# A graph-attention and graph-kernel pipeline over 16 pairs of batches: prologue in another order, x buffers by parity, last tiles finished one by one

## The reference

```python
def layer0(x, wq, wk, adj, bm):                     # attention over the 512 columns
    q, k = einsum('c,bcn->bn', wq, x), einsum('c,bcn->bn', wk, x)
    s = leaky(q[:, None, :] + k[:, :, None], 0.01)
    att = softmax(s, axis=-1)                       # 512 x 512 of each batch
    agg = einsum('bcn,bmn->bcm', x, att)
    return relu(einsum('oc,bcm->bom', adj, agg) + bm)

def layer1(h, adj, W_lang, W_grav, W_V, W_O):       # kernel over the 256 rows
    z_l, z_g, v = h @ W_lang.T, h @ W_grav.T, h @ W_V.T
    A_l = relu(cosine(z_l, z_l)) * not_eye          # 256 x 256 of each batch
    A_g = exp(-dist2(z_g, z_g) / (2 * sigma**2)) * not_eye
    K = w_l * rows_to_one(A_l * adj) + (1 - w_l) * rows_to_one(A_g * adj)
    return (K @ v) @ W_O.T

x = layernorm(x + layer0(x))
out = layernorm(x + layer1(x))
```

## Time and profile before

| what | value |
|---|---|
| median of three runs | 1048.47 us (1047.57 to 1049.12) |
| the profiled execution's own time | 1045.15 us |
| its span | 1043.4 us |
| TensorE busy | 1014.2 us, 97% |
| VectorE, ScalarE, GpSimd busy | 792.3 us (76%), 654.6 us (63%), 385.6 us (37%) |
| granted TensorE clock over the span | 0.996 of full speed |
| start to step 1 (0 to 143.31): TensorE busy | 124.88 us |
| steps 1 to 15 up to the last residual (143.31 to 1032.79): TensorE busy | 889.35 of 889.48 us |
| last residual to the end (1032.79 to 1043.40): TensorE busy | 0 of 10.61 us |

### The profile page before, as it was taken

The page is one execution under the profiler, slowest core; times in us unless marked ns, Lnnn a source line. Parts: engine busy times, 40 slices in busy tenths (PEclk is TensorE's granted clock), DMA queues, the critical chain, the costliest instruction groups (busy, mean ns, idle before and its releaser), DMA issues.

```text
span 1043.4 us, 19673 instructions
## 1 busy us (share of the span) xinstructions
PE 1014.2 (97%) x7189; PEld 695.5 (67%) x7189; DVE 792.3 (76%) x2318; ACT 654.6 (63%) x1267; POOL 385.6 (37%) x340
## 2 busy tenths in 40 slices
PE   7888999999999999999999999999999999999995
PEld 4465848577584857758485775848577584857662
DVE  5775776878787687878768787876878787787756
ACT  2658576665857666585766658576665857666432
POOL 0335334262533426253242625324262532424200
PEclk9999999999999999999999999999999999999998
DMA  7020221314022141402214140221414022131211
GB/s 271 32 82 1 32 91 52 112 41 107 16 75 88 48 116 41 114 10 72 91 47 117 41 113 10 71 92 46 118 41 106 18 69 94 44 79 41 41 41 41
DMA packets 85233, 72.05 MB, mean 69 GB/s; under 512 B 64144, under 2 KB 64656, under 8 KB 83088
## 3 DMA queue, kind: packets, MB, share of 16 engines
q1 hardware_dynamic: 85136, 70.79, 23.4%
HBM read 21.50 MB, written 16.78 MB: 37 GB/s over the span
## 4 chain that ended last, share of the span: by engine, by line
PE 84%; issue 5%; DVE 1%; ACT 1%; POOL 1%; POOLq 0%; DVEq 0%; ACTq 0%
PE bank L254 25%; PE bank L255 25%; PE bank L256 25%; PE bank L338 3%; PE bank L446 2%; PE bank L261 2%; PE bank L478 1%; POOL att_lo L1274 0%; DVE o L896 0%; ACT bank L578 0%; DVE t_lo L1069 0%; ACT t_hi L671 0%; ACT a_g L666 0%; ACT z_hi L655 0%; POOLq L63 0%
## 5 line engine op out<-in xcount | busy, mean ns | idle before, releaser
L1291 POOL TENSOR_TENSOR att_lo<-att,att_hi 128x512 f16<-128x512 f32 x128 | 148.2, 1158 | 337.4 <-ACT att_hi L584 337.4
L254 PE MATMUL bank<-xw_hi,att_hi 128*128 128x257 f16 x512 | 140.4, 274 | 1.2 <-DVE wvo_lo L858 1.0
L255 PE MATMUL bank<-ht_lo,z_hi 128*128 128x256 f16 x512 | 139.6, 273 | 0.0
L254 PE MATMUL bank<-ht_hi,z_hi 128*128 128x256 f16 x512 | 139.6, 273 | 0.0
L256 PE MATMUL bank<-ht_hi,z_lo 128*128 128x256 f16 x512 | 139.6, 273 | 0.0
L256 PE MATMUL bank<-xw_hi,att_lo 128*128 128x257 f16 x512 | 139.5, 272 | 0.0
L255 PE MATMUL bank<-xw_lo,att_hi 128*128 128x257 f16 x512 | 139.1, 272 | 0.0
L1043 DVE TENSOR_TENSOR z_lo<-bank,z_hi 128x512 f16<-128x512 f32 x128 | 88.2, 689 | 48.1 <-ACT z_hi L655 48.1
L603 ACT ACTIVATE agg_t<-bank,den_inv 128x256 f32<-128x256 f32 x128 | 58.4, 472 | 79.3 <-DVE den_inv L903 78.9
L1274 POOL TENSOR_TENSOR att_lo<-h,att_hi 128x512 f16<-128x512 f32 x60 | 67.6, 1159 | 102.3 <-DVE t_lo L1069 102.3
L683 ACT ACTIVATE z_hi<-bank 128x512 f16<-128x512 f32 x64 | 37.6, 591 | 95.6 <-PE bank L256 95.6
(11 more groups left out here) (177 smaller groups left out, 2629.3 us busy)
## 6 DMA issues: line engine op xcount, KB each, us to landing
x_in<-in_x SPq DMA_DIRECT2D x16, 1024.0 KB, 5.5
x_res<-x_in SPq DMA_DIRECT2D x16, 1024.0 KB, 5.1
out_y<-o SPq DMA_DIRECT2D x32, 512.0 KB, 2.8
agg_t<-in_wl SPq DMA_DIRECT2D x4, 256.0 KB, 3.5
y<-in_wg SPq DMA_DIRECT2D x1, 1024.0 KB, 9.3
o<-in_wv SPq DMA_DIRECT2D x1, 1024.0 KB, 11.5
h<-in_woT SPq DMA_DIRECT2D x1, 1024.0 KB, 13.6
att<-in_adjT SPq DMA_DIRECT2D x1, 256.0 KB, 4.0
```

The source lines that it names most:

```text
L254: pe.matmul(dst, ah, bh, start=(i == 0 and first), stop=False, skip_group_check=skip)
L255: pe.matmul(dst, ah, bl, start=False, stop=False, skip_group_check=skip)
L1291: pool.tensor_tensor(att_lo[:, n[0], n[1], :], att[:, g % 2, :], att_hi[:, n[0], n[1], :], ALU.subtract).then_inc(s["att_lo_done"], 1)
```

## The change

- `x_in` and `x_res` become two buffers by the parity of the pair (`x2`, read through `x_of`). The 16 copies within SBUF are gone; the load of x waits for the y of two pairs before, and for the split of it.
- `xw` becomes two buffers (`xw2`).
- Step -2: all rows of the first Gram, then the x products of pair 0, then the first row of the second Gram.
- Step -1: the rest of the second Gram and one value-output row, then the x products of pair 1, then the attention products of pair 0. VectorE's split of x of pair 1 and its xw_lo stand among the attention tiles of pair 0; the lower half of x (j = 1) is split by GpSimd behind the first att_lo.
- The four value-output rows leave their banks by ACT copies to SBUF (`wvo_raw`, in the buffers of a_l and a_g), and the scale and split are taken from there. Two of the rows stand between `turn_agg` and the transposes of h.
- Step 0 has an order of its own on each engine: two t products stand among the attention products; the value-output scale and the constants stand between two attention tiles; the four h tiles of pair 1 stand behind the second masked rows, ahead of `a_l_tiles` and of xw_lo 6.
- The end works by tile: statistics, mean, power (one column) and normalization of each tile for itself, three of the four normalizations on ACT with a shift and the rstd as scale, the last one on VectorE, and four stores of 256 KB.

The core of the diff:

```diff
-        x_res = sb("x_res", [2, CC, N])
+        turn_y, turn_o = sb("turn_y", [1]), sb("turn_o", [4])
+        o_shift = sb("o_shift", [4])
+        x2 = sb("x_in", [2, 2, CC, N])
...
-        xw_hi, xw_lo = sb("xw_hi", [2, NC, OW], F16), sb("xw_lo", [2, NC, OW], F16)
+        xw2_hi, xw2_lo = sb("xw_hi", [2, 2, NC, OW], F16), sb("xw_lo", [2, 2, NC, OW], F16)
...
-        wvo_bank = (7, 4, 5, 3)
+        wvo_bank = (4, 4, 4, 6)
+        first = (6, 7, 3, 1)
...
-                if l0 and p > -2:
-                    wait(sp, s["y_done"], 2 * q)
-                    wait(sp, s["y_odd_done"], 2 * q)
-                    wait(sp, s["x_loaded"], 16 * (q + 1))
-                    sp.dma_start(x_res[:], x_in[:]).then_inc(s["xr_loaded"], 16)
                 if new:
-                    wait(sp, s["x_lo_done"], 2 * r)
-                    wait(sp, s["xr_loaded"], 16 * r)
-                    sp.dma_start(x_in[:], x_v[r]).then_inc(s["x_loaded"], 16)
+                    if p >= 0:
+                        sp.wait_ge(s["x_lo_done"], 2 * q)
+                        sp.wait_ge(s["y_done"], 2 * q)
+                        sp.wait_ge(s["y_odd_done"], 2 * q)
+                    sp.dma_start(x_of(r), x_v[r]).then_inc(x_landed(r), 16)
...
+            for k in range(4):
+                sp.wait_ge(s["normed"], 2 * PAIRS - 1 + k)
+                sp.dma_start(out_v[PAIRS - 1, k // 2, :, k % 2:k % 2 + 1, :], o[:, k:k + 1, :]).then_inc(s["stored"], 16)
+            sp.wait_ge(s["stored"], 32 * PAIRS + 32)
...
+            def fuse_row(d):
+                if d > 0:
+                    pe.wait_ge(s["wvo_raw_done"], min(d, 2))
+                if d == DC - 1:
+                    pe.wait_ge(s["relu_done"], 1)
+                for f in range(DC):
+                    last = pe.matmul(bank[wvo_bank[d]][:], wv_raw[:, f, d * P:(d + 1) * P], wo_raw[:, f, :],
+                                     start=(f == 0), stop=(f == DC - 1))
+                last.then_inc(s["wvo_mm"], 1)
...
+                spread_top(5, (2, 3), s["top_l"])
                 k_rows(0)
+                pe.wait_ge(s["top_l_all"], 1)
+                gram_row(1, 1)
+                gram_row(1, 2)
+                pe.wait_ge(s["wv_loaded"], 16)
+                pe.wait_ge(s["wo_loaded"], 16)
+                pe.wait_ge(s["t_done"], 2)
+                fuse_row(0)
+                pe.wait_ge(s["u_lo_done"], 1)
+                gram_row(1, 3)
                 for k in range(8):
                     wx_product(k)
+                fuse_row(1)
+                for k in range(8):
+                    pe.wait_ge(s["att_lo_done"], 4 * (k // NC) + 4)
+                    if k == 0:
+                        pe.wait_ge(s["xw_lo_done"], 16)
+                    att_product(q, k)
+                    if k == 1:
+                        pe.wait_ge(s["wvo_raw_done"], 2)
+                        spread_top(4, (3, 4), s["top_g"])
+                turn_agg(q)
+                pe.wait_ge(s["u_lo_done"], 2)
+                k_rows(1)
+                fuse_row(2)
+                fuse_row(3)
+                pe.wait_ge(s["t_done"], 3)
                 pe.wait_ge(s["h_done"], 4)
                 for d in range(DC):
...
+                        if at(p, 0) and k == 3:
+                            t_product(0)
+                            t_product(1)
...
+            def wvo_raw_row(d):
+                act.wait_ge(s["wvo_mm"], d + 1)
+                act.activation(wvo_raw[d], bank[wvo_bank[d]][:], ACT.Copy).then_inc(s["wvo_raw_done"], 1)
...
+            def o_mean_tile(pair, k):
+                dve.wait_ge(s["o_stat_done"], 4 * pair + k + 1)
+                dve.tensor_scalar(turn_o[:, k:k + 1], o_stat[:, k, 0:1], 1.0, None, ALU.mult)
+                dve.bn_aggr(o_mv[:, k, :], o_stat[:, k, :]).then_inc(s["o_mv_done"], 1)
+            def o_shift_tile(pair, k):
+                dve.wait_ge(s["o_rstd_done"], pair + k + 1)
+                dve.wait_ge(s["o_mv_done"], pair + k + 1)
+                dve.scalar_tensor_tensor(out=o_shift[:, k:k + 1], in0=o_mv[:, k, 0:1], scalar=-1.0,
+                                         in1=o_rstd[:, k:k + 1], op0=ALU.mult, op1=ALU.mult)\
+                    .then_inc(s["o_shift_done"], 1)
+            def o_norm_last(pair, k):
+                dve.wait_ge(s["o_rstd_done"], pair + k + 1)
+                dve.wait_ge(s["o_mv_done"], pair + k + 1)
+                dve.wait_ge(s["normed"], 2 * pair + k)
+                dve.tensor_scalar(o[:, k, :], o[:, k, :], o_mv[:, k, 0:1], o_rstd[:, k:k + 1],
+                                  ALU.subtract, ALU.mult).then_inc(s["normed"], 1)
...
+                    gram_top(0)
                     return
+                gram_scales(0)
                 t_rows(0)
+                u_lo(0)
+                dve.wait_ge(x_landed(1), x_count(1))
+                dve.wait_ge(s["wx_mm"], 8)
+                dve.tensor_copy(x_hi[:, 0], x_of(1)[:, 0]).then_inc(s["x_hi_done"], 1)
+                att_tile(q, 0)
+                dve.wait_ge(s["x_hi_done"], 3)
+                dve.tensor_tensor(x_lo[:, 0], x_of(1)[:, 0], x_hi[:, 0], ALU.subtract).then_inc(s["x_lo_done"], 1)
+                dve.tensor_copy(x_hi[:, 1], x_of(1)[:, 1]).then_inc(s["x_hi_done"], 1)
+                att_tile(q, 1)
+                xw_lo_tile(p, 0)
+                att_tile(q, 2)
+                xw_lo_tile(p, 1)
+                xw_lo_tile(p, 2)
+                att_tile(q, 3)
+                xw_lo_tile(p, 3)
+                xw_lo_tile(p, 4)
+                att_tile(q, 4)
+                gram_top(1)
+                xw_lo_tile(p, 5)
+                xw_lo_tile(p, 6)
+                att_tile(q, 5)
+                xw_lo_tile(p, 7)
+                q_tops(r)
+                att_tile(q, 6)
                 den(q, 0)
...
                 y_stat_tile(q, 3)
                 y_mean(q)
+                t_rows(1, (0,))
                 for k in range(4):
                     h_tile(q, k)
+                t_rows(1, (1,))
+                wvo_top((2,))
                 for d in range(DC):
                     dve.wait_ge(s["ht_hi_done"], d + 1)
                     dve.tensor_tensor(ht_of(0)[1][:, :, d, :], bank[d][:].rearrange("p (k n) -> p k n", k=4),
                                       ht_of(0)[0][:, :, d, :], ALU.subtract)\
                        .then_inc(s["ht_lo_done"], 1)
...
+                if at(p, 0):
+                    for k in range(4):
+                        h_tile(1, k)
...
                     residual(k)
+                    if not l0:
+                        o_stat_tile(p, k)
+                        o_mean_tile(p, k)
+                        if k > 0:
+                            o_shift_tile(p, k - 1)
...
+            o_norm_last(PAIRS - 1, 3)
...
+                        if at(p, -1) and g == 0:
+                            pool.wait_ge(s["x_hi_done"], 4)
+                            pool.wait_ge(s["x_lo_done"], 3)
+                            pool.tensor_tensor(x_lo[:, 1], x_of(1)[:, 1], x_hi[:, 1], ALU.subtract)\
+                                .then_inc(s["x_lo_done"], 1)
...
             pipeline(step)
+            for k in range(4):
+                pool.wait_ge(s["o_mv_done"], PAIRS + k)
+                pool.tensor_tensor(o_var[:, k:k + 1], o_mv[:, k, 1:2], eps[:, k:k + 1], ALU.add)\
+                    .then_inc(s["o_var_done"], 1)
+                pool.wait_ge(s["o_var_done"], PAIRS + k)
+                wait(pool, s["normed"], 2 * PAIRS - 2)
+                pool.tensor_tensor(o_rstd[:, k:k + 1], o_var[:, k:k + 1], exponent[:, k:k + 1], ALU.pow)\
+                    .then_inc(s["o_rstd_done"], 1)
```

370 lines of the change are left out of this document (205 added, 165 removed).

## The result

The changed kernel took 1034.55 us in the median of four runs (1033.71 to 1035.44), the kernel before 1048.02 (four runs, 1045.34 to 1049.12): ratio 0.9875, interval 0.9854 to 0.9896, a gain of 13.5 us. In a second look of four runs it took 1033.92, ratio 0.9863 (0.9846 to 0.9879). The forecast was 1039.2 with a range from 1034.5: the sign is right, the time lies only 0.05 us inside the lower end of the range, and the gain is 4.2 us larger than the sum of 9.3.

A forecast was written before the change was run, and what follows sets the result against it. TensorE bounds steady stretches, so gains lie in 18.0 us lost ahead of step 1 and the 10.6 us end. 6.5 + 2.8 = 9.3 us off the median 1048.47 gives 1039.2, range 1034.5 to 1043.5.

The forecast's parts named there:

- The median, 3.32 above it: Whole kernel: the median lies 3.32 us above the profiled execution's 1045.15, so 1048.47 less 9.3 gives 1039.2.
- the ledger ahead of step 1: TensorE before step 1: 14.5 us of listed waits, 1.8 hidden and 1.7 of low clock, 18.0 us in all.
- The prologue: Everything ahead of step 1: 11.4 us of losses remain against 18.0, so step 1 starts some 6.5 us earlier.
- x_lo of the second pair: Step -1: TensorE waits 1.8 us, 35.7 to 37.5, for the lower half of x split by GpSimd.
- products 5 and 7: Step -1, second pair's x products: TensorE waits 0.4 + 1.6 us for xw_lo queued behind held-up attention tiles.
- att_lo in step 0: Step 0: attention products wait 1.4 us, as VectorE has 1.7 us of scales and constants between second and third tile.
- The end: Behind the last residual: work by tile gains 1.9 us to the last normalization and 0.9 at the store, 2.8 together.
- The shared port: Step -1: GpSimd and VectorE hold each other up; an attention tile takes 0.7 us alone, 1.57 beside att_lo.
- the port costs nothing: Rival, chance 0.20: the first wait terms shrink from 6.6 to 2.65 us, gain 13.3, time 1035.2.
- Ties and low clock: Rival, chance 0.14: GpSimd goes first at two places, 1.1 us each, and low clock costs 1.7; time 1043.1.
- Waits didn't only move: Rival, chance 0.07: VectorE and ACT queues give back all 18.0 us, leaving only the end's gain; time 1045.7.
- the steady steps waited for no load: Slower rival, chance 0.05: x loads delay ht_lo, TensorE loses 0.9 us in each of 14 steps; time 1051.8.

The follow-up runs named there:

- The second look: The kernel before run once more, unchanged: 1047.65 us, ratio 1.0002; its profiled execution took 1048.14 us.
- eight transposes: Kernel before with eight transposes of the identity into an unused bank ahead of the first Gram row: 1047.49 us, ratio 0.9997.
- later h: The changed kernel with the four h tiles of step 0 behind xw_lo 6 and 7 instead of ahead of the a_l tiles: 1036.29 us, ratio 0.989.

## Why the prediction was right in sign and too small

**What failed: the step from the profiled execution to the median.** "The median, 3.32 above it" was carried over as a constant. It was none. The execution on which the sum rests had drawn well twice: its first Gram row took 5.09 us (5.29 to 6.67 in the four other traces of before and its variants without work ahead of it), and no low clock followed its wait for x_lo (one did in the four other traces that have that wait). The second look, with 1048.14 near the median of 1048.02, differs from it by 1.31 us for the one and 1.66 for the other. The first is a draw of both kernels (5.31 to 6.61 us in the change and its variants) and no gain of the change. The second is a gain, for the change has no wait for x_lo of the first pair; the ledger ahead of step 1 had no term for the clock behind that wait.

What it had was 1.7 for the stretch behind ul_lo. As time that passed in that execution this is right; as a gain by itself it was worth nothing, since the attention products start 14.33 us behind that wait with the stretch and without. Low clock at such a wait is a draw: in the traces of before and its variants 13 of the 17 waits of 2.3 to 2.6 us have 3.4 us at 0.50 with them (one of three in the trace, three of three in the second look, two of three with the end alone, three of three with x by parity and with eight transposes, one of two with the first Gram whole); the one wait of 2.44 in the variant with later h has it, too. In the seven other traces of the change and its variants, whose longest wait behind the first weights is 1.44, none has. Why one wait brings it and an equal one doesn't stays open.

As an estimate from these numbers: the 9.3 of the sum, 1.1 more at the end, 2.0 for smaller waits (both below) and 1.7 for the clock behind x_lo make 14.1, against 13.5 measured.

**The 9.3 us: 10.3 in the profiled executions.** *The prologue*, 6.5 forecast, 6.43 measured, but that they agree is luck: two errors cancel. The waits left over came to 9.4 instead of 11.4, and the later first Gram row took back 1.9. The forecast terms hold the 0.16 us that the list hides in each wait, so the last column is the one to compare:

| wait | forecast | listed | with 0.16 each |
|---|---|---|---|
| x_lo of the second pair | 1.8 | 0.98 | 1.14 |
| products 5 and 7 | 0.4 + 1.6 | none, 1.19 | 1.35 |
| attention products | 1.6 | 1.44 | 1.60 |
| the turn of the aggregate (reciprocals) | 0.65 | 0.51 | 0.67 |
| h | 0.55 | 0.30 | 0.46 |
| ht_lo | 0.95 | 0.74 | 0.90 |
| att_lo in step 0 | 1.4 | 0.88 | 1.04 |
| xw_lo there (three forecast, two came) | 0.9 | 0.57 | 0.89 |
| second value product | 1.4 | 1.21 | 1.37 |
| the turn | 0.1 | none | none |

No wait came at a place that was not named. Too large were x_lo, products 5 and 7 and att_lo, by 0.36 to 0.66; the others are met within 0.1. *The end*, 2.8 forecast, 3.87 measured (the end alone confirms it): the last residual came 0.97 late instead of 1.35, the power on one column took 0.55 and not the 1.01 of four, and the last store gave 1.25 instead of 0.9. *x by parity*, nothing forecast, nothing measured. *The shared port*: the row was kept and not the rule for a whole duration, and the row was right (a cast and two tiles end 0.54 to 0.55 behind GpSimd's); the terms that hung on it, 4.0 us by the rival "no cost", cost 3.0 to 3.5 with GpSimd's own time.

**The rivals.** The measured 1034.55 lies next to the time of "the port costs nothing" (1035.2), yet the trace shows the port's cost at every place: a right-looking time by a wrong cause. "Ties and low clock" expected low clock in the change; none came, and no wait in it behind the first weights was over 1.44 us. Waits didn't only move, and the steady steps waited for no load (890.45 us against 889.48, the difference being the last residual).

## What to carry to other kernels

Before the difference of two traces is added to a median, look at how an execution differs from its fellows: where a kernel has waits that may or may not bring a lower clock, one trace shows one draw. Count a stretch of low clock as a loss only where nothing behind it gives it back: the one behind x_lo cost 1.66 us, those at ul_lo and z_lo nothing, since there VectorE set the pace and TensorE's later waits shrank by as much. Where GpSimd works from SBUF, give VectorE the work whose input lies in PSUM for that time.

## What was not expected of the hardware

Waits of the same 2.3 to 2.6 us bring the 1.2 GHz level in one execution and not in the next, and of the three places of the prologue where it came, it cost time at one only. The first matmuls after the start go at half pace though the granted clock reads 1.00 there, and at full pace with eleven small products ahead of them (a row in 3.60 us instead of 6.61). A cast with one SBUF input is held up by GpSimd just as a tile with two (0.45 to 1.33 us).
